# Cross attention: the maximum of each query taken from the scores themselves, and the scores kept in 21 SBUF tiles until it is known

## What is computed

```python
q = _rms_norm((draft_hidden @ Wq.T).reshape(bsz, draft_len, H, HD), q_norm_w)
kv_in = jnp.concatenate([context_hidden, draft_hidden], axis=1)
k = _rms_norm((kv_in @ Wk.T).reshape(bsz, total_len, KVH, HD), k_norm_w)
v = (kv_in @ Wv.T).reshape(bsz, total_len, KVH, HD)
q, k = _rope(q, draft_position_ids), _rope(k, full_position_ids)
scores = jnp.einsum('bhqd,bhkd->bhqk', q, k) * SCALE      # 4 query heads share a key head
probs = jax.nn.softmax(scores, axis=-1)
attn = jnp.einsum('bhqk,bhkd->bhqd', probs, v)
return attn @ Wo.T
```

## Time and profile before

| | before |
|---|---|
| time, median of 3 runs | 1749.54 us (1746.96 to 1752.52) |
| time of the profiled execution | not given beside the runs |
| span of the profiled execution, first to last instruction | 1746.4 us |
| busy in the span | PE 1567.7, DVE 1320.0, POOL 1141.2, ACT 814.5 us |
| granted TensorE clock, mean | 0.965 |

### The profile page before, as it was taken

How to read it: one execution, slowest core, us unless ns; L and a number is a source line. 1 busy time by engine, 2 the same in 40 slices (tenths; PEclk the granted TensorE clock), 3 DMA queues, 4 the chain that set the end, 5 groups by cost and what they waited for, 6 DMA issues and landing times. The chain is left out here.

```text
span 1746.4 us, 27001 instructions
## 1 busy us (share of the span) xinstructions
PE 1567.7 (90%) x8692; PEld 910.2 (52%) x8692; DVE 1320.0 (76%) x2642; ACT 814.5 (47%) x1975; POOL 1141.2 (65%) x1069
## 2 busy tenths in 40 slices
PE   6597796776779999999999999999999999999987
PEld 5476464533434555554555555455555555554454
DVE  7876577878787888788687777968877787776554
ACT  3363664651445454443545444454544444444352
POOL 2362570132667799787779978777987777866642
PEclk9799898978999999999999999999999999999999
DMA  3000820010100000100000100000000000000010
GB/s 97 1 2 30 284 87 25 1 69 0 51 0 13 1 13 1 51 1 1 1 1 1 39 1 1 1 1 1 1 19 1 1 1 1 1 1 1 1 55 25
DMA packets 28498, 38.54 MB, mean 22 GB/s; under 512 B 4804, under 2 KB 24776, under 8 KB 28360
## 3 DMA queue, kind: packets, MB, share of 16 engines
q1 hardware_dynamic: 28360, 36.82, 6.3%
HBM read 35.76 MB, written 1.05 MB: 21 GB/s over the span
## 5 line engine op out<-in xcount | busy, mean ns | idle before, releaser
L2141 POOL TENSOR_TENSOR stream_acc<-stream_acc,stream_p 128x512 f32<-128x512 f32 x448 | 577.0, 1293 | 180.0 <-ACT stream_p L2029 179.0
L2029 ACT ACTIVATE stream_p<-stream_lowered 128x512 f32<-128x512 f32 (+1 forms) x480 | 302.6, 631 | 588.8 <-DVE stream_lowered L2204 584.1
L1964 PE MATMUL stream_banks<-stream_p,stream_v 128*128 128x512 f32 (+1 forms) x960 | 491.5, 594 | 5.5 <-ACT stream_p L2029 5.5
L2204 DVE TENSOR_TENSOR stream_lowered<-stream_banks,stream_shift_all 128x512 f32<-128x512 f32 (+1 forms) x480 | 329.3, 686 | 123.7 <-PE stream_banks L1951 109.8
L2211 DVE TENSOR_REDUCE stream_tops<-stream_banks 128x1 f32<-128x512 f32 (+1 forms) x512 | 324.7, 636 | 95.9 <-PE stream_banks L1937 93.9
L1964 PEld LDWEIGHTS stream_banks<-stream_p,stream_v 128*128 128x128 f32 (+1 forms) x960 | 182.2, 190 | 76.3 <-ACT stream_p L2029 8.0
L1937 PE MATMUL stream_banks<-stream_k_t_hi,stream_q_t_hi 128*128 128x512 bf16 (+1 forms) x512 | 183.7, 360 | 22.1 <-DVE stream_tops L2211 21.0
L1951 PE MATMUL stream_banks<-stream_q_t_hi,stream_k_t_hi 128*128 128x512 bf16 (+1 forms) x480 | 183.0, 381 | 0.0
L1951 PE MATMUL stream_banks<-stream_q_t_lo,stream_k_t_hi 128*128 128x512 bf16 (+1 forms) x480 | 181.9, 379 | 0.0
L1951 PE MATMUL stream_banks<-stream_q_t_hi,stream_k_t_lo 128*128 128x512 bf16 (+1 forms) x480 | 181.9, 379 | 0.0
L2148 POOL TENSOR_TENSOR stream_by_cos<-stream_by_cos,stream_by_sin 128x256 f32<-128x256 f32 x192 | 133.6, 718 | 34.0 <-DVE stream_by_sin L2237 33.8
(11 more groups left out here) (431 smaller groups left out, 2878.2 us busy)
## 6 DMA issues: line engine op xcount, KB each, us to landing
memory_raw_t<-in_ctx_t SPq DMA_DIRECT2D x4, 1601.0 KB, 8.9
row_ctx_t<-in_ctx_t SPq DMA_DIRECT2D x4, 1601.0 KB, 7.3
memory_raw<-in_ctx SPq DMA_DIRECT2D x4, 1536.0 KB
early_raw<-in_L_xattn_Wq SPq DMA_DIRECT2D x4, 512.0 KB, 3.9
stream_raw_o<-in_L_xattn_Wo SPq DMA_DIRECT2D x4, 512.0 KB, 3.8
moe_raw_up<-in_L_ffn_wi SPq DMA_DIRECT2D x6, 256.0 KB, 4.3
model_x<-in_x SPq DMA_DIRECT2D x1, 1024.0 KB, 5.4
self_sm<-in_L_ffn_w_fc SPq DMA_DIRECT2D x1, 1024.0 KB, 6.8
```

Source lines behind the costliest of these rows:

```text
L1964: nc.tensor.matmul(ps[:, 2 + n, :], v[0:r, g % 2, t, :], p32[0:r, step % 4, :], start=(t == 0), stop=(t == KT - 1)).then_inc(weighed, 1)
L2029: nc.scalar.activation(p32[0:r, step % 4, :], lowered[0:r, step % 3, :], ACT.Exp, scale=SCALE).then_inc(p32_ready, 1)
L2141: nc.gpsimd.tensor_tensor(acc[0:r, g % 2, cols], acc[0:r, g % 2, cols], p32[0:r, step % 4, :], ALU.add).then_inc(acc_ready, 1)
L2204: nc.vector.tensor_tensor(lowered[0:r, step % 3, :], ps[0:r, step % 2, :], shift_all[0:r, g % 2, n * HALF:(n + 1) * HALF], ALU.add).then_i ...
```

## The change

The pieces go, and with them `tops`, `shift_all` and `p32`. A group is now worked in two **passes**, one for each half (`PASSES` = 32, `STEPS` = 15, so a step is still one tile against one half, and there are still 480). In the slot of a step the scores are made as before. VectorE takes a running maximum over the key tiles, from the bank (`keep_most`, L2207 in the changed file, `most`, 128x512). ScalarE **then** copies the bank to one of 21 tiles in SBUF (`copy_scores`, L2036; 16 of `weights` and rows of `ctx_t` that the context no longer holds), and that copy frees the bank. After 15 steps TensorE transposes `most` (4 matmuls), VectorE reduces it (`take_top`, L2213), and TensorE and ScalarE turn and spread the negated maximum into bank 7. 18 slots after the scores (`LOWER`) VectorE adds bank 7 to the tile in place (L2195) and ScalarE takes the exponential in place (L2042). One slot later (`WEIGH` = 19) TensorE weighs it and GpSimd adds it up.

Preparation now starts 27 slots ahead (32 for the first six units). `vary` (variance from the sum of squares, 128x4) moves from ScalarE to VectorE. k and q tiles lose one buffer each, and the context is loaded in chunks. Sums, inverses and projections come once a pass, for two heads each.

```diff
-STEPS = HALVES * KT
+STEPS = KT
+PASSES = GROUPS * HALVES
-AHEAD = 55
+AHEAD = 27
+LOWER = STEPS + 3
+WEIGH = LOWER + 1
+ROOMS = 21
...
-                    if step >= 2:
-                        pe.wait_ge(lowered_ready, step - 1)
+                    if step >= 2:
+                        pe.wait_ge(copied, step - 1)
...
+                def copy_scores(step):
+                    h, g, n, t = step_of(step)
+                    r = rows_of(t)
+                    ac.wait_ge(maxed, step + 1)
+                    if step >= ROOMS:
+                        ac.wait_ge(weighed, step - ROOMS + 1)
+                        ac.wait_ge(acc_ready, step - ROOMS + 1)
+                    nc.scalar.copy(room(step)[0:r], ps[0:r, step % 2, :]).then_inc(copied, 1)
...
                 for slot in SLOTS:
                     if 0 <= slot < ALL:
-                        exponent(slot)
+                        copy_scores(slot)
+                    if 0 <= slot - LOWER < ALL:
+                        exponent(slot - LOWER)
...
                     if 0 <= slot < ALL:
                         score(slot)
-                    pieces = pieces_in(slot)
-                    if 0 <= slot - BEHIND < ALL:
-                        weigh(slot - BEHIND)
-                    for item in pieces[:1]:
-                        piece(item)
+                    if 0 <= slot - WEIGH < ALL:
+                        weigh(slot - WEIGH)
+                    for h in pass_at(slot, TOPS_LATE):
+                        turn_most(h)
...
+                def keep_most(step):
+                    h, g, n, t = step_of(step)
+                    r = rows_of(t)
                     ve.wait_ge(scored, step + 1)
+                    if t == 0:
+                        if h >= 1:
+                            ve.wait_ge(most_turned, h)
+                        nc.vector.tensor_copy(most[:], ps[:, step % 2, :]).then_inc(maxed, 1)
+                    else:
+                        ve.wait_ge(maxed, step)
+                        nc.vector.tensor_tensor(most[0:r], most[0:r], ps[0:r, step % 2, :], ALU.max).then_inc(maxed, 1)
...
                 for slot in SLOTS:
-                    if 0 <= slot < ALL:
-                        lower(slot)
+                    if 0 <= slot - LOWER < ALL:
+                        lower(slot - LOWER)
...
-                    for item in pieces_in(slot):
-                        reduce_piece(item)
                     for u in units_at(slot, 3):
                         rotate(u, 0)
+                        if unit(u)[1] < QT:
+                            vary(u)
                     for u in units_at(slot, 6):
                         if unit(u)[1] >= QT:
                             rotate(u, 1)
+                            vary(u)
+                    if 0 <= slot < ALL:
+                        keep_most(slot)
+                    for h in pass_at(slot, TOPS_LATE):
+                        take_top(h)
```

More of the change, by code:

```diff
@@ L1549, in start_of @@
 def start_of(u):
-    return EVERY * u - AHEAD
+    return EVERY * u - AHEAD - (EVERY if u < UNITS else 0)
 def turn_of(u):
-    return start_of(u) + 2 * EVERY - 1 + (EVERY if u < 7 else int(u == 7))
+    return start_of(u) + 2 * EVERY - 1 + (EVERY if u < UNITS else 0)
 def units_at(slot, late):
-    n, rest = divmod(slot - late + AHEAD, EVERY)
-    return [n] if rest == 0 and 0 <= n < UNITS * GROUPS else []
+    return [u for u in range(UNITS * GROUPS) if start_of(u) + late == slot]
 def turns_in(slot):
@@ L1572, in last_use, with pass_at, outs_in @@
     return start_of(UNITS * (KVH * row - 1) + i)
[L1575 to L1587, removed]
+def pass_at(slot, late):
+    h, rest = divmod(slot - late, STEPS)
+    return [h] if rest == 0 and 0 <= h < PASSES else []
+TOPS_LATE, FLAT_LATE, SPREAD_LATE = STEPS, STEPS + 1, STEPS + 2
+ATT_LATE = STEPS + WEIGH
+SUM_LATE = ATT_LATE + 1
+def outs_in(slot):
     found = []
[L1589 to L1592, removed]
-    return found
[L1596 to L1607, removed]
+    for m in range(PAIR):
+        found += [(h, m) for h in pass_at(slot, SUM_LATE + (1, 4)[m]) if h < PASSES - 1]
+        found += [(h, m) for h in pass_at(slot, SUM_LATE + 1) if h == PASSES - 1]
+    return found
 def ctx_span(chunk):
@@ new lines, in turn_top, with spread @@
+                def turn_top(h):
+                    pe.wait_ge(top_ready, h + 1)
+                    wait_bank6("flat", h)
+                    nc.tensor.matmul(ps[0:4, 6, 0:P], top[:], const["ident_b"][:], start=True, stop=True).then_inc(top_turned, 1)
+                def spread(h):
+                    pe.wait_ge(flat_ready, h + 1)
+                    if h >= 1:
+                        pe.wait_ge(lowered, STEPS * h)
+                    for c in range(4):
+                        last = nc.tensor.matmul(ps[:, 7, c * P:(c + 1) * P], own[:, c, :], flat[:], start=True, stop=True)
+                    last.then_inc(spread_ready, 1)
@@ L1983, in project_out, with sum_up @@
-                def project_out(g, n):
-                    if g < GROUPS - 1:
-                        wait_bank(("out", g, n))
+                def sum_up(h):
+                    wait_bank6("sum", h)
+                    pe.wait_ge(acc_ready, STEPS * (h + 1))
+                    for c in range(4):
+                        last = nc.tensor.matmul(ps[:, 6, c:c + 1], acc[:, h % 2, c * P:(c + 1) * P], ones[:], start=True, stop=True)
+                    last.then_inc(sum_ready, 1)
+                def project_out(h, m):
+                    g, n = divmod(h, HALVES)
+                    if h < PASSES - 1:
+                        wait_bank6("out", (h, m))
@@ L2100, in _ @@
                             take_values(u, 1)
-                            vary(u, 1)
+                    for h in pass_at(slot, FLAT_LATE):
+                        flatten(h)
                     for u in turns_in(slot):
                         high(u)
-                    for item in sides_in(slot):
-                        if item[0] != "sum":
-                            spread_shift(item)
+                    g, late = divmod(slot, HALVES * STEPS)
                     if g == GROUPS - 1 and late == 8:
@@ L2207, in reduce_piece @@
[L2207 to L2215 removed]
+                        ve.wait_ge(spread_ready, h + 1)
```

371 lines of the change are left out of this document (170 added, 201 removed).

## The result

| | before | after |
|---|---|---|
| median | 1749.12 us (1746.96 to 1752.52, 4 runs) | 1961.36 us (1959.32 to 1965.17, 4 runs) |
| ratio, 95% interval | | 1.1207 (1.118 to 1.1234) |
| span of the profiled execution | 1746.4 us | 1961.1 us |
| granted TensorE clock, mean | 0.965 | 0.952 |

What follows compares the result with a forecast made beforehand. TensorE bounds the old kernel; after the change it waits on a 2.34 us loop from scores to exponential. Terms 466 + 32 + 1287 + 43 + 62 + 28 + 91 give 2009, called 2010 us, range 1860 to 2090.

Steps and rivals of the forecast that it cites:

- (1): Start: only six units stand ahead of the first score, so it comes at about 466 us, not 497.3.
- (3) and (4): Slots 19 to 451 at 2.97 us each, 1287 us, plus 43 us for new batch rows and output weights.
- The group: 30 slots of the stream: 67 us TensorE work, 20.7 of waits, 1.5 for `vary`, 89.2 us; range 83 to 92.
- The walk: Step through a group's 30 slots with assumed durations, listing TensorE's waits before weighing: 20.7 us in 18 slots.
- `vary`: Tiny VectorE variance operation, moved from ScalarE, in six units a group: 0 to 3 us more, 1.5 taken.
- The signs: Trace marks expected: no L1937 or L2211, first score near 466, about 20 us of TensorE waits before weighing a group.
- rival C: New waits bring TensorE stretches at 1.2 GHz in each group: 2085 to 2200 us; chance 0.12.
- Rows and weights: Three new batch rows, which block ScalarE and VectorE, and the output weights: 43 us, ends 20 and 60.
- The tail: 19 slots at the end, GpSimd longest at 1.27 us each, and the last projection: 28 us.
- Rival A: TensorE's work decides because the 2.34 us loop is hidden: faster, 1647 us; chance 0.08.
- Rival B: Only half of the waits, a group near 78 us: whole time 1760 to 1890 us; chance 0.13.
- D: No change in time, for which A and B would have to meet; chance 0.02.

Runs made afterwards that it cites:

- all three edits: Changed kernel with ScalarE's exponential before its copy, VectorE's running maximum before low, rotate and vary, and the weighing one slot later: 1691.48 us, 0.9676.
- the three edits: Each alone on the changed kernel: weighing one slot later, 1783.21 us; exponential before copy on ScalarE, 1755.58 us; maximum before rotation on VectorE, 1811.79 us.
- fewer pieces: Kernel before the change, with the subtracted value taken from the first 512 keys only, 8 pieces a group instead of 32: 1679.92 us, 0.961.
- two edits: Changed kernel with exponential before copy on ScalarE and running maximum before low, rotate and vary on VectorE: 1712.28 us, 0.9796.

## Why the prediction was right, point by point

The forecast was 2010, the result 1961 us, and the mechanism was the one named. By its own terms:

| term | predicted | measured | |
|---|---|---|---|
| (1) first score | 466 | 458.1 | -8 |
| (2) slots 0 to 18 | 32 | 36.1 | +4 |
| (3) and (4) slots 19 to 451 with rows and weights | 1287 + 43 | 1273.6 | -56 |
| (5) slots 452 to 479 | 62 | 63.4 | +1 |
| (6) tail | 28 | 38.5 | +10 |
| (7) behind the stream | 91 | 91.4 | 0 |

**The group** was put at 89.2 us and takes 86.4. The walk had waits in 18 slots, 20.7 us in all. By the distances from the last score matmul to the weighing the trace has them in 15 slots, and each of the 15 is one of the walk's, in us:

| slot | 1 | 2 | 4 | 7 | 9 | 11 | 12 | 16 | 17 | 19 | 22 | 24 | 26 | 27 | 29 |
|---|---|---|---|---|---|---|---|---|---|---|---|---|---|---|---|
| walk | 1.1 | 1.9 | 0.7 | 1.6 | 0.7 | 1.6 | 2.8 | 1.1 | 1.2 | 0.9 | 0.3 | 1.7 | 1.0 | 1.3 | 1.0 |
| measured | 0.9 | 1.5 | 0.5 | 1.9 | 0.4 | 1.3 | 2.6 | 0.9 | 0.8 | 0.5 | 0.9 | 1.5 | 0.7 | 1.1 | 0.7 |

Slots 8, 14 and 23, 1.8 us of the walk, have none. The two longest stand behind the rotations of the two query units, as said, and maximum to maximum at a query unit was put at 4.3 and takes 4.17. With some tenths in small ones the waits are 16.3 us, so 4.4 less than walked, and nothing is left in them for the 1.5 of `vary`. What remains is 86.4 - 16.3 = 70.1 against 67 of work: a clock of 0.98 makes up some 1.7 us of the difference, and with all three edits, when no weighing waits, the group takes 68.3, so the work was put about 1.3 too low. The group came out closer than its terms, because these errors have opposite signs.

**The signs.** L1937 and L2211 are gone. VectorE waits 64.5 us for squares before the rotation (57 times) and 35.1 us for scores before the maximum. One sign was off: the first score came 8 us earlier than said, at 458.1. And one sign against the forecast showed itself in part, the stretches at half clock (rival C, below).

**`vary`** was the term with the widest ends, nothing to 3 us a group, and 1.5 was taken. It costs the low end (one line: count, then ns minimum, median, maximum):

```profile
L2241 DVE TENSOR_SCALAR stream_var<-stream_ss x96: 158/160/868, 443.4 to 1774.9; 128x4 f32<-128x4 f32 x80, 128x3 f32<-128x3 f32 x16
```

The median is 0.16 us, not the 0.62 of the earlier trace rows; only single ones reach 0.87. By the rule of SBUF — State Buffer, section "SBUF: two separate sides", in the Trainium skill, such an instruction, if it runs in a two-port mode, could have waited for a whole GpSimd operation; in this kernel, with GpSimd busy 64 of 86 us, most did not wait. Six of them at 0.16 make about 1 us a group, 0.4 more than the walk had: term 1.1 too high.

**Rows and weights** were counted at 43 us; 1273.6 less 433 slots at 86.4/30 is 26.6. The middle group is a low one to reckon from; others take 85.3 to 94.1. A group with a new batch row takes some 6.5 us more than it (93.0 and 92.8), where in the kernel before it took some 8.5 more. That its stalls fell partly where TensorE stood anyway would explain this; it was not tested.

**The tail** was sized by GpSimd's 1.27 us a step, 24 of the 28 us, and this term was too small (order of time, changed kernel):

```profile
1854.87 8.30 POOL L2136 TENSOR_TENSOR stream_acc<-stream_acc,stream_weights 128x512 f32<-128x512 f32 x6
1863.32 1.84 PE L1986 MATMUL stream_banks<-cross_ones,stream_acc 128*128 128x1 f32 x8 [4.18 <-POOL stream_acc L2136]
```

Six additions end 8.30 us after the first one's start: each is 1.27 long, but they start 1.41 apart. In the kernel before, three back to back take 3.74 (from 1635.15), 1.23 apart. The code has a reason that the prediction missed: an addition waits for the one before it on the same half (`acc_ready`); before, that was two steps back, and with passes it is the last one. No run tested this by itself. For 19 steps it makes 2.7 us; GpSimd also waits 5.0 us for exponentials in the tail, so it ends its last sum 32.0 us after the last slot of scores, not 24. TensorE waits 4.18 us for that sum and runs the rest at half clock (a window from 1862 us on has 0.50): 6.5 us to the end instead of 4.

**Rival C, the clock,** had a part. Two windows just behind the middle group show it:

```profile
1420.00:1424.00 4.00, 2.23 (x5) 0.73 (x6) 1.76 (x3) 2.71 (x8) 3.42 (x5) 0.69 0.01 2
1424.00:1428.00 4.00, 4.00 (x13) 2.09 (x12) 2.61 (x5) 1.12 (x3) 1.66 (x2) 0.50 0.02 6
```

In the first TensorE is busy 2.23 of 4 us, and the granted clock falls; in the second it is at 0.50, 1.2 GHz, and TensorE, now busy throughout, gets 13 matmuls done. By the records of the granted clock slots 19 to 451 hold 11 such stretches, 47.8 us together, against 2 with 6.8 us in the stream before (the prediction had seen one of these, at 841; the other starts at 1140). That is 3.3 us in a group of 30 slots, half of the two of 3.4 that rival C assumed. A matmul takes at most twice as long in them, so they cost at most half of the 41 us more, 20 us of the 212. That ceiling was worked out, not tested by itself. The forecast's reading, that the waits would mostly leave the clock, held: 0.98 in this part.

**Rival A** fell for this order of queues, and its work was nearly right: the condition that the prediction gave for it ("if the exponential stood at least a slot earlier", or the rotation not between two maxima) is what the experiments made true, and the group then takes 68.3 us, against the rival's 67. **Rival B** fell: the waits are 4.4 us shorter than walked, not half. **D** fell by far. The range of the group, 83 to 92, is not what its three named ends give around 89.2 (84.7 to 92.7 us); the measured group lies in both.

One part of the reading was tested harder than the rest: each of the three edits alone removes 150 to 206 of 212 us, so they do not add up. That is what a loop does: it is closed only if all of its links hold, and opening any one of them lets most of it go.

Two means lead under the 1749 us of before: fewer pieces (1680 us), and the new order of queues (1712 us with two edits, 1691 with all three). What the last one still has of waits (the scores for their bank, the spread of the maxima at L1968, the copies for GpSimd's sum to free a tile, GpSimd's lag at the tail) was left as it is; no kernel was tried that removes those.

## What to carry to other kernels

When engines work through fixed queues, look for a cycle: what is the newest product that an old, urgent instruction stands behind? Sum the durations once around and set them beside the bound engine's work for the same distance; totals of busy time, which here all had room, say nothing of it. Put the consumer of the oldest data first in each queue, or give the hand-over one slot more: the 21 tiles were enough for it. With all three edits they begin to be short; ScalarE's copies of the scores then stand about 26 us for GpSimd to free a tile, where in the changed kernel they do not.

## What the runs showed of the hardware

- A tiny VectorE instruction from SBUF (128x4) took 0.16 us in the median beside a GpSimd that was busy 64 of 86 us in a group, where another of its kind had 0.62. Why these differ stays open.
- TensorE was granted 1.2 GHz for some microseconds 11 times in a part in which it was busy 83% of the time (1051.93 of 1273.60 us). Ahead of one of them, at 1363 us, it had waited 1.16 and 2.40 us within 5 us. Another of that size, 1.74 us at 1348, has no such stretch behind it; which do stays open.
- ScalarE's copy of 128x512 from a bank took 0.586 us on average and the next instruction could start 0.48 us behind it (1002.25 to 1002.73); the forecast had 0.63 and 0.53 for the same.
- GpSimd's addition of 128x512 into a sum was recorded 1.27 us long in both kernels; back to back the additions started 1.41 us apart where each waited for the one just before, and 1.23 where it waited for the one before that.
